# Turning two more units in blocks at the end of an attention and expert kernel

## The reference, cut to what matters

```python
x = layernorm(x + first_attention(x))             # one head of width 256, causal
h = layernorm(x, ln1); q, k, v = h @ wq + bq, h @ wk + bk, h @ wv + bv     # 16 heads of 128
probs = softmax(mask(rope(q) @ rope(k).T / sqrt(128)))
h = x + (probs @ v) @ wo + bo
m = layernorm(h, ln2)                             # gate: softmax, best 2 of 4
out = h + sum_e comb[:, e] * (gelu(m @ we1[e] + be1[e]) @ we2[e] + be2[e])
out = layernorm(x + out)
```

## Time and profile before

| | before |
|---|---|
| three executions | 1060.58, 1060.66, 1062.13 us; median 1060.66 us |
| profiled execution | 1061.71 us, its span 1059.6 us |
| TensorE busy | 1040.0 us (98%), granted clock 0.996 of full speed |
| VectorE, ScalarE, POOL busy | 764.5, 809.6, 638.5 us |
| transfers of the exchange | 336 of 256 KB, 4.7 to 4.8 us from issue to landing |

### The profile page before, as it was taken

One profiled execution on the slowest core, in us unless ns is written; L12 is line 12 of the kernel. 1 busy time (PEld: TensorE's weight loads), 2 busy tenths in 40 slices (PEclk: granted clock), 3 DMA queues, 4 the chain that ended last, 5 costly groups with the idle time before them and its releaser, 6 DMA issues.

```text
span 1059.6 us, 16929 instructions
## 1 busy us (share of the span) xinstructions
PE 1040.0 (98%) x5636; PEld 853.0 (81%) x5636; DVE 764.5 (72%) x1725; ACT 809.6 (76%) x1376; POOL 638.5 (60%) x516
## 2 busy tenths in 40 slices
...
GB/s 185 1 1 45 56 30 146 135 136 131 134 120 145 120 135 119 145 122 141 125 153 130 144 129 148 129 143 126 156 124 147 127 110 1 11 110 1 41 1 80
DMA packets 61174, 110.85 MB, mean 105 GB/s; under 512 B 7072, under 2 KB 11296, under 8 KB 61088
## 3 DMA queue, kind: packets, MB, share of 16 engines
...
q10 hardware_dynamic: 144, 0.03, 0.0%
...
## 4 chain that ended last, share of the span: by engine, by line
PE 90%; ACT 3%; POOL 2%; DVE 2%; issue 2%; DMA 1%; SPq 1%; POOLq 0%; DVEq 0%; ACTq 0%
PE ps_s L489 24%; PE ps_m L489 23%; PE ps_t L489 15%; PE ps_t L676 14%; PE ps_m L676 6%; PE ps_m L652 3%; PE ps_m L668 3%; PE ps_t L639 1%; ACT prob_b L1266 1%; SPq L2577 1%; PE ps_m L536 1%; DMA work<-in_attn_w 0%; DMA we<-pT 0%; POOL acc L2360 0%; POOL qk_lo L2365 0%
## 5 line engine op out<-in xcount | busy, mean ns | idle before, releaser
L2315 POOL TENSOR_TENSOR work<-work,rope 128x512 f32<-128x512 f32 x128 | 164.8, 1288 | 244.8 <-ACT work L1217 244.0
L1842 DVE CUSTOM_DVE_ANT_0 ps_s<-ps_s,causal 128x128 f32<-128x128 f32 (+7 forms) x272 | 207.2, 762 | 91.9 <-PE ps_s L489 87.0
L1266 ACT ACTIVATE prob_b<-ps_s,nmax 128x640 f32<-128x640 f32 (+3 forms) x136 | 225.4, 1657 | 33.9 <-DVE nmax L1842 33.7
L2326 POOL TENSOR_TENSOR qk_lo<-work,qk_hi 128x512 fp32r<-128x512 f32 x128 | 167.4, 1313 | 35.9 <-ACT qk_hi L1223 35.9
L2319 POOL TENSOR_TENSOR work<-work 128x512 f32<-128x512 f32 x128 | 166.6, 1302 | 11.7 <-DVE work L1809 1.8
L676 PE MATMUL ps_t<-we,values 128*128 128x512 f32 (+3 forms) x432 | 164.0, 512 | 0.0
L489 PE MATMUL ps_s<-qk_hi 128*128 128x384 f32 (+5 forms) x384 | 155.9, 406 | 2.1 <-ACT prob_b L1266 2.1
L489 PE MATMUL ps_s<-qk_hi,qk_lo 128*128 128x384 f32 (+5 forms) x384 | 131.5, 343 | 0.0
L489 PE MATMUL ps_s<-qk_lo,qk_hi 128*128 128x384 f32 (+5 forms) x384 | 131.2, 342 | 0.0
L1858 DVE STREAM_TRANSPOSE pT<-prob_b 128x640 f32<-128x640 f32 (+1 forms) x112 | 116.5, 1040 | 16.9 <-ACT prob_b L1266 16.9
L1266 ACT ACTIVATE prob_s<-ps_s,nmax 128x128 f32<-128x128 f32 (+3 forms) x136 | 109.4, 807 | 16.0 <-DVE nmax L1842 15.3
...
## 6 DMA issues: line engine op xcount, KB each, us to landing
...
```

The lines of the kernel that those rows point to most:

```text
L1266: act.activation(to, scores_, ACT.Exp, bias=nmax[:, u % 2, i:i + 1], scale=-1.0, accum_out=rsum[:, u % 2, i:i + 1]).then_inc(exp_done.sem, ...
L1842: dve.tensor_tensor_reduce(s, s, causal[:, T - (i + 1) * P:T], -1.0, ABOVE_ALL, ALU.add, ALU.min, accum_out=nmax[:, u % 2, i:i + 1]).then_ ...
L2315: pool.tensor_tensor(qs[:, x, :], qs[:, x, :], sin_t[:, c * CH:(c + 1) * CH], ALU.mult).then_inc(sin_done.sem, sin_done.up(u, x))
L2326: pool.tensor_tensor(qk_lo[:, u % 2, j, cols], qc[:, ring3(u, x), :], qk_hi[:, u % 2, j, cols].bitcast(F32), ALU.subtract).then_inc(qk_lo_ ...
```

## The change

Units 31 and 32 are turned in blocks too, so only 0, 1, 2 and 33 are left to TensorE's transposes. The loop of heads runs one turn longer (to head(31)). The turn buffer for c = 0 is turn0, of its own; early_pT, the moved one, lies in mids, the place of the last expert's middle values. turn0 is also where copy_p puts the turned tiles 0 to 3 of unit 33, and VectorE clears it in start(), between row_max(0, 6) and row_max(0, 7). turn_probs(3, 0) no longer waits for the layer norm. The pieces of expert weights come in the order m = 1, then m = 2. ends() has a new order on all engines. What comes behind the parts shown is as before.

```diff
-TURNED = range(3, LAST - 2)
+TURNED = range(3, LAST)
...
-        early_pT = sb("early_pT", [P, TC, CH])
+        early_pT = mids_[:, :, :, :].rearrange("p a b n -> p (a b) n").bitcast(F32)
+        turn0 = sb("turn0", [P, TC * CH])
...
-        turned = (shared_ln[:, :], pT[:, :, :].rearrange("p j n -> p (j n)"))
+        turned = (turn0[:, :], pT[:, :, :].rearrange("p j n -> p (j n)"))
...
-        we_pieces = [(m, e) for m in (2, 1) for e in range(EXPERTS)]
+        we_pieces = [(m, e) for m in (1, 2) for e in range(EXPERTS)]
...
+        def pT_of(u, c):
+            return turn0[:, :].rearrange("p (j n) -> p j n", n=CH) if (u, c) == (LAST, 0) else pT[:, TC * (1 - c):, :]
...
+            def two_banks():
+                recent[:] = [n for n in recent if n < 2]
...
             start()
-            for u in TURNED:
+            for u in TURNED[:-1]:
                 head(u)
             ends()
...
+            def clear_early_turns():
+                dve.memset(turn0[:, :], 0.0).then_inc(pT_cleared, 1)
...
-                if (u, i) == (TURNED[0], 0):
-                    dve.wait_ge(ln_mm.sem, ln_mm.at(3, 1, KD - 1))
-                    dve.wait_ge(hT_lo_pool.sem, hT_lo_pool.at(3, 1, KD - 1))
```

TensorE:

```diff
 def ends():
+    project_q(LAST, 0)
+    project_q(LAST, 1)
+    scores(LAST - 1, 4)
+    far_outputs(LAST - 2, 0)
+    scores(LAST - 1, 5)
+    far_outputs(LAST - 2, 1)
+    scores(LAST - 1, 6)
+    near_outputs(LAST - 2)
+    scores(LAST - 1, 7)
+    bias_row()
+    out_project(LAST - 2, 1, 0)
+    scores(LAST, 0)
+    project_q(LAST, 2)
+    scores(LAST, 1)
+    out_project(LAST - 2, 1, 1)
+    project_q(LAST, 3)
+    early_outputs(LAST - 1)
+    scores(LAST, 2)
+    scores(LAST, 3)
+    out_project(LAST - 1, 0, 0)
+    out_project(LAST - 1, 0, 1)
+    two_banks()
+    transposes(LAST, 0)
+    transposes(LAST, 1)
+    far_outputs(LAST - 1, 0)
+    scores(LAST, 4)
+    transposes(LAST, 2)
+    far_outputs(LAST - 1, 1)
+    scores(LAST, 5)
+    near_outputs(LAST - 1)
+    transposes(LAST, 3)
+    scores(LAST, 6)
+    transposes(LAST, 4)
+    out_project(LAST - 1, 1, 0)
+    out_project(LAST - 1, 1, 1)
+    ln_transpose(4, 0)
+    scores(LAST, 7)
+    outputs(LAST, 0)
+    transposes(LAST, 5)
+    gate_products(0, 0)
+    out_project(LAST, 0, 0)
+    out_project(LAST, 0, 1)
+    ln_transpose(4, 1)
+    gate_logits(0, 0)
+    transposes(LAST, 6)
+    gate_products(0, 1)
+    transposes(LAST, 7)
+    gate_logits(0, 1)
+    expert_in(0, 0)
+    expert_in(0, 1)
+    outputs(LAST, 1)
...
```

ScalarE:

```diff
 def ends():
+    high_gates()
+    high_bias_row()
+    add_bias(LAST, 0)
+    add_bias(LAST, 1)
+    exponent(LAST - 1, 4)
+    high_qk(LAST, 0)
+    exponent(LAST - 1, 5)
+    high_qk(LAST, 1)
+    high_o(LAST - 2, 1)
+    exponent(LAST - 1, 6)
+    exponent(LAST - 1, 7)
+    add_bias(LAST, 2)
+    exponent(LAST, 0)
+    add_bias(LAST, 3)
+    high_o(LAST - 1, 0)
+    exponent(LAST, 1)
+    high_qk(LAST, 2)
+    exponent(LAST, 2)
+    high_qk(LAST, 3)
+    exponent(LAST, 3)
+    copy_p(LAST, 0)
+    copy_p(LAST, 1)
+    exponent(LAST, 4)
+    high_expert(1, 0)
+    copy_p(LAST, 2)
+    copy_p(LAST, 3)
+    high_o(LAST - 1, 1)
+    exponent(LAST, 5)
+    high_expert(1, 1)
+    exponent(LAST, 6)
+    copy_p(LAST, 4)
+    ln_affine(4, 0)
+    high_o(LAST, 0)
+    copy_p(LAST, 5)
+    gate_rows(0, 0)
+    exponent(LAST, 7)
+    high_expert(1, 2)
+    ln_affine(4, 1)
+    copy_p(LAST, 6)
+    high_expert(1, 3)
+    gate_rows(0, 1)
+    copy_p(LAST, 7)
+    gate_exps(0, 0)
+    high_expert(2, 0)
+    gelu_mid(0, 0)
+    high_mid(0, 0)
+    gelu_mid(0, 1)
+    gelu_mid(0, 2)
+    high_expert(2, 1)
+    high_mid(0, 1)
+    gate_exps(0, 1)
+    gelu_mid(0, 3)
+    high_mid(0, 2)
+    high_expert(2, 2)
+    high_o(LAST, 1)
+    high_mid(0, 3)
+    high_expert(2, 3)
+    ln_rows(5, 0)
...
```

VectorE:

```diff
 def ends():
+    rotate(LAST, 0)
+    row_max(LAST - 1, 4)
+    rotate(LAST, 1)
+    invert(LAST - 1, 0)
+    row_max(LAST - 1, 5)
+    turn_probs(LAST - 1, 4)
+    row_max(LAST - 1, 6)
+    turn_probs(LAST - 1, 5)
+    low_o(LAST - 2, 1)
+    row_max(LAST - 1, 7)
+    turn_probs(LAST - 1, 6)
+    add_bias_row()
+    row_max(LAST, 0)
+    accumulate(LAST - 2, 1, 0)
+    turn_probs(LAST - 1, 7)
+    rotate(LAST, 2)
+    rotate(LAST, 3)
+    accumulate(LAST - 2, 1, 1)
+    row_max(LAST, 1)
+    low_o(LAST - 1, 0)
+    row_max(LAST, 2)
+    row_max(LAST, 3)
+    accumulate(LAST - 1, 0, 0)
+    accumulate(LAST - 1, 0, 1)
+    invert(LAST - 1, 1)
+    invert(LAST, 0)
+    ln_stats(4, 0)
+    row_max(LAST, 4)
+    ln_apply(4, 0)
+    ln_stats(4, 1)
+    row_max(LAST, 5)
+    low_o(LAST - 1, 1)
+    row_max(LAST, 6)
+    accumulate(LAST - 1, 1, 0)
+    accumulate(LAST - 1, 1, 1)
+    row_max(LAST, 7)
+    low_o(LAST, 0)
+    ln_apply(4, 1)
+    accumulate(LAST, 0, 0)
+    accumulate(LAST, 0, 1)
+    gate_copy(0, 0)
+    gate_copy(0, 1)
+    gating_1(0)
+    gating_2(0)
+    invert(LAST, 1)
+    ln_stats(5, 0)
+    ln_apply(5, 0)
+    low_o(LAST, 1)
...
```

POOL:

```diff
 def ends():
+    low_gates()
+    low_bias_row()
+    turn(LAST, 0)
+    turn(LAST, 1)
+    low_qk(LAST, 0)
+    low_qk(LAST, 1)
+    turn(LAST, 2)
+    turn(LAST, 3)
+    low_qk(LAST, 2)
+    low_qk(LAST, 3)
+    add_row(0, 0)
+    add_row(0, 1)
+    ln_power(4, 0)
+    ln_power(4, 1)
+    ln_low(4, 0)
+    low_expert(1, 0)
+    low_expert(1, 1)
+    ln_low(4, 1)
+    low_expert(1, 2)
+    low_expert(1, 3)
+    add_row(1, 0)
+    low_expert(2, 0)
+    low_mid(0, 0)
+    low_mid(0, 1)
+    low_expert(2, 1)
+    low_expert(2, 2)
+    low_mid(0, 2)
+    low_mid(0, 3)
+    low_expert(2, 3)
+    ln_power(5, 0)
+    add_row(1, 1)
...
```

SyncE:

```diff
 def ends():
+    load_expert(1, 0)
+    load_expert(1, 1)
+    exchange(LAST - 1, 1)
+    exchange(LAST - 1, 2)
+    load_expert(1, 2)
+    load_be2()
+    load_x1(0, 0)
+    load_expert(1, 3)
+    load_expert(2, 0)
+    load_x1(0, 1)
+    load_expert(2, 1)
+    load_expert(2, 2)
+    load_expert(2, 3)
...
```

More of the change, by code:

```diff
@@ L665, in outputs @@
                     off = max(0, j - TC * c) * P
-                    slot = j + (4 if c == 0 else 0)
                     vals = slice(h * HD, (h + 1) * HD)
-                    last = pe.matmul(out[:, off:CH], values[:, s, j, vals], pT[:, slot, off:CH], start=j == 0,
+                    last = pe.matmul(out[:, off:CH], values[:, s, j, vals], pT_of(u, c)[:, j, off:CH], start=j == 0,
                                      stop=j == tiles - 1)
@@ L962, in ends @@
-                scores(LAST - 1, 1)
-                out_project(LAST - 2, 0, 1)
-                scores(LAST - 1, 2)
-                transposes(LAST - 2, 7)
-                project_v(VALUES - 1, 3)
-                outputs(LAST - 2, 1)
-                transposes(LAST - 1, 0)
-                project_q(LAST, 0)
-                scores(LAST - 1, 3)
-                transposes(LAST - 1, 1)
-                scores(LAST - 1, 4)
+                project_q(LAST, 0)
+                project_q(LAST, 1)
```

229 lines of the change are left out of this document (15 added, 214 removed).

## The result

The changed kernel is slower by 0.27% (95% interval 0.20 to 0.33%), little, but clear of no change.

What follows compares the result with a forecast made beforehand. TensorE, busy 1040.0 of 1059.6 us, bounds the kernel. Transposes −8.0, old waits −4.9 and new waits +12.8 sum to −0.1 us on a base of 1060.66: 1060.5 us, no change (chance 0.40), range 1054.5 to 1064.5.

Steps and rivals of the forecast that it cites:

- rival (b): Slower, chance 0.24: wait 6 grows to 4.8 us and TensorE's clock falls behind it, costing 1.7 us; 1063.6 us.
- wait 6: TensorE's wait at unit 33's end, before out_project(33, 1, 0), for VectorE's low_o: 3.5 us (2.9 to 4.8).
- the start: The turn0 clearing, 1.8 us on VectorE, delays first_outputs(0, 1, 0) by at most 0.5 us; costed at nothing.
- The transposes: Taking the turns of units 31 and 32 off TensorE saves 4.0 us a unit, 8.0 us for two.
- Wait 1: TensorE before out_project(32, 0, 0), waiting for low_o, with 0.3 us for early scores(33, 0): 1.0 us (0.1 to 1.5).
- Wait 2: TensorE before far_outputs(32, 0), waiting for the exchange of unit 32's blocks: 2.6 us (1.0 to 3.6).
- Waits 3 to 6: TensorE at layer norm transposes 1.0, gate_products(0, 1) 3.0, expert_in(0, 1) behind gelu 1.7, out_project(33, 1, 0) 3.5 us.
- Rival (a): Faster, chance 0.36: the waits at the end do not add up but shrink to 6.8 us; 1054.6 us.
- the clock: TensorE's clock in the new end: no loss in the sum; only rival (b) had it fall, for 1.7 us.
- the old waits: TensorE's waits between the loop of heads and the first product of experts, 4.9 us, go.

Runs made afterwards that it cites:

- e12: Kernel with clearing first, ln_power(5, 0) early and high_expert(2, 0) behind the first gelu, plus far_outputs(32, 0) ahead of transposes(33, 0) and (33, 1): 1056.41 us.
- e1: Changed kernel with the clearing of turn0 as VectorE's first work instead of behind row_max(0, 6): 1062.59 us, ratio 1.0009.
- e3: Kernel before with only a memset of 2048 columns added on VectorE behind row_max(0, 6): 1062.29 us, ratio 1.0008.
- e11: Changed kernel with 22 idle transposes of the identity on TensorE behind expert_out(0, 0, 0) alone: 1061.89 us, ratio 1.0006.
- e9: Changed kernel with 59 idle transposes on TensorE, 37 in earlier waits of the end and 22 behind expert_out(0, 0, 0): 1061.89 us, ratio 1.0012.
- e4: Changed kernel with the clearing of turn0 as VectorE's first work and ln_power(5, 0) behind low_mid(0, 1) on POOL: 1057.97 us, ratio 0.996.

## Why the prediction was wrong

The forecast was 1060.5, no change; what came is rival (b), slower: 1063.7 against its 1063.6. That the two numbers meet is partly luck: (b) has wait 6 at 4.8 us, which was 3.8, nothing for the start, and a base 0.9 us under the 1061.56 of these runs.

**The transposes** gave 7.3 us of 8.0. **Wait 1** was 0.68 of 1.0.

**Wait 2** was to be 2.6 us and is nothing. The terms of the exchange held nearly: the transfers start 5.0 us after scores(32, 7) (5.3 forecast; 903.81 to 908.82) and need 8.12 (8.66, by e12), 13.1 us together. The changed kernel's TensorE arrives after 13.2 us (903.81 to 916.96), not 11.3. What was missing are 0.92 us of waits for the accumulate in front of transposes(33, 0) and (33, 1), which the sum did not have, and 1.2 us of work: without its 1.60 us of waits TensorE needs 11.5 us there, where 10.3 were counted. So the wait is missing because two errors of the sum on TensorE's side happened to reach just as far as the exchange needs. The Trainium skill, "DMA: Bandwidth & Descriptors", section "Anatomy of one DMA — SWDGE (gpsimd) path", has 2.0 us plus bytes over 436 GB/s for the other issuing path, from which the prediction had estimated 4.4 us. That is not what the 1 MB took here: e12 shows 8.12 from issue to go on.

**Waits 3 to 6** were 1.4 (1.0 forecast), 2.2 (3.0), 2.4 (1.7) and 3.8 (3.5) in size, and of the last 2.8 were seen. With the unforeseen 0.25 and 0.92 all waits are 11.7 us against 12.8. Walking along each queue was good to about one microsecond in all, in part by luck, since wait 2 was 2.6 us too high and the unforeseen ones made up for 1.2 of it. Rival (a), that the waits melt to 6.8 us, was wrong.

**The first step that failed is the start.** "row_max(0, 7), which stands between, waits for its own scores as well, so I take nothing". It had waited 0.60 us and was pushed by 1.76 us, and then by a microsecond more, for bqk beside POOL. Cost: about 1.0 us (1.15 by e1's median, 0.8 by e3's, 0.9 of wait in the profiles), against a bound of 0.5. The bound went by the gap in front of low_first(1, 0) and left out what stands in the queue between the memset and it.

**The second, and the larger, is the clock.** The sum put it at nothing, and the prediction had it only in rival (b), against "the row of 865 to 870, where the clock stayed at 1.00 with 1.33 us idle". Every run of the changed kernel lies at 0.991 to 0.997, over half of before at 0.999. Filling wait 6 with idle products takes off 1.85 us (e11), and 1.7 us was the price worked out from the row of 160 to 165. In the one profile of the changed kernel the fall lies in front of wait 6 and costs 0.6 us; behind wait 6, where (b) expected it, only e1's profile has it, for 1.4. How the rest of the 1.85 us comes about stays open. The clock falls to 1.2 GHz in the profiles behind waits of 2.41 us (changed, 0.73 in the row of 950) and 3.81 us (e1, 0.88 and 0.78 in the rows of 960 and 965). The Trainium skill, "TensorE: Matmul & The Clock Gate", section "Part 1: The HAM clock gate (the "warmup" mystery)", had throttled as the default that activity must lift; the trace agrees by these two rows, and it should have weighed more: a row with one wait of 1.52 us does not speak for a stretch that is to have waits of 2.4 and 3.8.

Together: −7.3 for the transposes, −4.9 for the old waits, +11.7 for the new ones and +1.0 for the clearing are +0.5 us. That is the change without the clock, and e11 and e9, with wait 6 filled, measure +0.6 (−0.2 to 1.6) and +1.3 (0.2 to 2.2). With the 1.85 us that e11 takes off it is +2.4 us; the ratio of the changed kernel gives 2.9 (2.1 to 3.5), the medians 2.2.

Two moved instructions, the clearing and ln_power(5, 0), make of the loss a gain: 1057.97 (e4), 0.4% under the kernel before. The change was right in its idea and lost what it won to where these two stood.
